# A Macaron block on one core: in steady passes the last shared chunk of a feed-forward layer is made behind the eleven expert chunks

## The reference

```python
x = x + 0.5 * ffn(_layernorm(x))          # pass f=0
x = x + mamba(_layernorm(x))              # state-space scan, 256 inner channels, 16 states
x = x + 0.5 * ffn(_layernorm(x))          # pass f=1, the same weights
```

```python
h = silu(einsum('tc,ech->eth', xf, W1)) * einsum('tc,ech->eth', xf, W2)
y = einsum('eth,ehc,te->tc', h, W3, w)    # w: the router's weight of each expert for a token
hs = silu(xf @ Ws1) * (xf @ Ws2)
y = y + (hs @ Ws3)
```

## Time and profile before

| | before |
|---|---|
| median of 3 runs | 1810.48 us (1804.98 to 1814.09) |
| the profiled execution | 1817.71 us |
| its span | 1816.0 us |
| mean granted TensorE clock | 0.975 |
| busy: PE, DVE, ACT, POOL | 1652.8, 1489.5, 1267.4, 1443.4 us |

### The profile page before, as it was taken

The page is one execution under the profiler, slowest core; times in us unless marked ns, Lnnn a source line. Parts: engine busy times, 40 slices in busy tenths (PEclk is TensorE's granted clock), DMA queues, the critical chain, the costliest instruction groups (busy, mean ns, idle before and its releaser), DMA issues.

```text
span 1816.0 us, 24043 instructions
## 1 busy us (share of the span) xinstructions
PE 1652.8 (91%) x7378; PEld 997.4 (55%) x7378; DVE 1489.5 (82%) x2244; ACT 1267.4 (70%) x2032; POOL 1443.4 (79%) x1362
## 2 busy tenths in 40 slices
PE   7878788999999999999999999999999999976689
PEld 4544445556565555556555555655555565543346
DVE  3177989889898988989798988989898898978862
ACT  3387678787868777776867777787777868585522
POOL 5256778888888888888888888889898888887853
PEclk9999889999999999999999999999999999988899
DMA  6127668686867778586777867777686868667732
GB/s 182 43 86 171 152 160 203 154 203 155 201 169 182 186 164 202 152 194 171 184 180 171 201 158 190 179 185 187 158 209 152 198 162 196 166 163 180 162 88 76
DMA packets 120999, 302.97 MB, mean 167 GB/s; under 512 B 19267, under 2 KB 40486, under 8 KB 106662
## 3 DMA queue, kind: packets, MB, share of 16 engines
q0 software_dynamic: 18144, 124.26, 34.2%
q1 hardware_dynamic: 100214, 175.36, 33.6%
q10 hardware_dynamic: 2512, 1.81, 0.3%
HBM read 167.67 MB, written 5.24 MB: 95 GB/s over the span
## 4 chain that ended last, share of the span: by engine, by line
POOL 45%; DMA 20%; issue 14%; PE 10%; DVE 8%; ACT 3%; SPq 1%; POOLq 0%; DVEq 0%; ACTq 0%
DMA yacc<-prod 18%; POOL prod L730 18%; POOL gated L661 14%; POOL yacc L726 3%; DVE hist L1023 3%; PE ps_y L1201 3%; DVE ps_db L978 2%; PE ps_h1a L1185 1%; PE ps_h2a L1209 1%; POOL yacc L747 1%; PE ps_h1b L1185 1%; PE ps_h2b L1209 1%; POOL xres L717 1%; POOL rstd L642 1%; POOL stdr L645 1%
## 5 line engine op out<-in xcount | busy, mean ns | idle before, releaser
L730 POOL TENSOR_TENSOR prod<-hist,crow 128x1024 f32<-128x1024 f32 x224 | 556.1, 2482 | 214.6 <-DVE hist L1023 183.8
L1201 PEld LDWEIGHTS ps_y<-down_w,gated 128*128 128x128 f32 (+1 forms) x3584 | 474.1, 195 | 278.9 <-issue 169.1
L1023 DVE TENSOR_TENSOR_SCAN hist<-decay,ps_db 128x1024 f32<-128x1024 f32 x256 | 583.5, 2279 | 3.0
L661 POOL TENSOR_TENSOR gated<-gated,silu 128x512 f32<-128x512 f32 x352 | 492.7, 1444 | 77.8 <-DVE gated L1003 74.3
L1201 PE MATMUL ps_y<-down_w,gated 128*128 128x128 f32 (+1 forms) x3584 | 489.1, 281 | 53.1 <-POOL gated L661 51.5
L978 DVE TENSOR_TENSOR ps_db<-du,ps_db 128x1024 f32<-128x1024 f32 x256 | 313.2, 1224 | 124.6 <-PE ps_db L1164 122.7
L791 ACT ACTIVATE decay<-delta,a_neg 128x510 f32<-128x510 f32 x512 | 326.8, 709 | 1.5
L808 ACT ACTIVATE silu<-ps_h1a 128x512 f32<-128x512 f32 (+1 forms) x224 | 133.0, 594 | 185.7 <-PE ps_h1a L1185 185.3
L1185 PE MATMUL ps_h1b<-xnT,up_w 128*128 128x512 f32 x448 | 238.6, 615 | 3.3 <-ACT silu L808 3.3
L1209 PE MATMUL ps_h2a<-xnT,up_w 128*128 128x512 f32 (+1 forms) x448 | 234.6, 606 | 6.6 <-DVE gated L1003 6.6
L1185 PE MATMUL ps_h1a<-xnT,up_w 128*128 128x512 f32 (+1 forms) x448 | 237.7, 612 | 0.0
(11 more groups left out here) (138 smaller groups left out, 1936.8 us busy)
## 6 DMA issues: line engine op xcount, KB each, us to landing
yacc<-prod POOLq DMA_DIRECT2D x111, 1024.0 KB, 9.8
crow<-c_rows SPq DMA_DIRECT2D x128, 512.0 KB, 5.0
wrow<-w_rows SPq DMA_DIRECT2D x320, 128.0 KB, 6.2
wrow<-w_rows SPq DMA_DIRECT2D x64, 224.0 KB, 7.1
wrow<-w_rows SPq DMA_DIRECT2D x64, 192.0 KB, 5.1
wrow<-w_rows SPq DMA_DIRECT2D x64, 160.0 KB, 2.8
yacc<-yacc POOLq DMA_DIRECT2D x15, 512.0 KB, 7.7
wrow<-w_rows SPq DMA_DIRECT2D x64, 96.0 KB, 2.9
```

The lines of the kernel that those rows point to most:

```text
L661: nc.gpsimd.tensor_tensor(gated[:, pos % NGATE, :], gated[:, pos % NGATE, :], silu[:, (pos + NCHUNK * f_parity(of, f)) % NSILU, :], ALU.mu ...
L730: nc.gpsimd.tensor_tensor(prod[:, (pair - 1 + odd) % 2, s % 2, :, :], hist[:, s % 2, :, :], c_all, ALU.mult).then_inc(prod_done, 1)
L1023: nc.vector.tensor_tensor_scan(hist[:, s % 2, :, :].rearrange("p h t -> p (h t)"), decay[:, s % NA, :, :, :].rearrange("p h b t -> p (h b ...
L1201: ins = nc.tensor.matmul(ps_y[:, t * C:(t + 1) * C], gated[0:rd, posd % NGATE, t * P:(t + 1) * P], down_w[0:rd, jd, :], start=(posd == 0 a ...
```

## The change

In f=0 passes of groups entering in iterations 2 to 13, and in f=1 passes of iterations 2 to 14, a second order holds: chunks 11 and 12, then the eleven expert chunks, then chunk 13. Expert chunk e now stands at place e + 2, and the 96 rows of chunk 13 at p13. All other passes keep the order of before. `UNIT`, `PLAN` and `SP_PLAN`, and so the slot of every place and the order of SP's list, stay as they are. The semaphore counts for the reuse of `wrow` and `silu`, and those that PE waits for, are worked out from the new order.

```diff
-    ORDER = list(range(ECHUNK, NCHUNK)) + list(range(ECHUNK))
+    SHARED_FIRST = list(range(ECHUNK, NCHUNK)) + list(range(ECHUNK))
+    ONE_SHARED_LAST = list(range(ECHUNK, NCHUNK - 1)) + list(range(ECHUNK)) + [NCHUNK - 1]
+
+    def order(it, f):
+
+        return SHARED_FIRST if it < FULL or (f and it >= G - 1) else ONE_SHARED_LAST
...
+    CHUNKS = [(it, f, j) for it, f in PASSES for j in order(it, f)]
+    def experts_of(n):
+        return sum(j < ECHUNK for _, _, j in CHUNKS[:n])
+    def taken_with(of, f, e):
+        return CHUNKS.index((of, f, e)) + 1
+    EXPERTS = [(it, f, j) for it, f, j in CHUNKS if j < ECHUNK]
...
-                n = fcount(k, f, NCHUNK, e if e >= NW else e - (NCHUNK - ECHUNK))
-                if n > 0:
-                    sp.wait_ge(h2_taken, n)
+                n = EXPERTS.index((k, f, e)) - NW
+                if n >= 0:
+                    sp.wait_ge(h2_taken, taken_with(*EXPERTS[n]))
...
-                    if u is not None and ORDER[u[2]] < ECHUNK:
+                    if u is not None and order(u[0], u[1])[u[2]] < ECHUNK:
...
-                        shared = NCHUNK - ECHUNK
-                        if NSILU <= pos < NSILU + shared:
+                        if n >= NSILU and CHUNKS[n - NSILU][2] >= ECHUNK:
                             act.wait_ge(h2_taken, n - NSILU + 1)
                         elif n >= NSILU:
-                            act.wait_ge(weighted, fcount(of, f, ECHUNK, pos - shared - (NSILU - 1 if pos >= NSILU else 0)))
+                            act.wait_ge(weighted, experts_of(n - NSILU + 1))
...
-                            pe.wait_ge(weighted, fcount(of, fd, ECHUNK, jd + 1))
+                            pe.wait_ge(weighted, experts_of(fcount(of, fd, NCHUNK, posd + 1)))
```

More of the change, by code:

```diff
@@ L799, in body @@
                         of, f, pos = u
-                        r = rows(ORDER[pos])
+                        r = rows(order(of, f)[pos])
                         n = fcount(of, f, NCHUNK, pos)
                         act.wait_ge(h1_full, n + 1)
-                        shared = NCHUNK - ECHUNK
-                        if NSILU <= pos < NSILU + shared:
+                        if n >= NSILU and CHUNKS[n - NSILU][2] >= ECHUNK:
                             act.wait_ge(h2_taken, n - NSILU + 1)
                         elif n >= NSILU:
-                            act.wait_ge(weighted, fcount(of, f, ECHUNK, pos - shared - (NSILU - 1 if pos >= NSILU else 0)))
+                            act.wait_ge(weighted, experts_of(n - NSILU + 1))
                         nc.scalar.activation(silu[0:r, (pos + NCHUNK * f_parity(of, f)) % NSILU, :],
@@ L989, in body @@
                         of, f, pos = u
-                        j = ORDER[pos]
+                        j = order(of, f)[pos]
                         r = rows(j)
@@ L1189, in body @@
                         of, fd, posd = d
-                        jd = ORDER[posd]
+                        jd = order(of, fd)[posd]
                         rd = rows(jd)
                         if jd < ECHUNK:
-                            pe.wait_ge(weighted, fcount(of, fd, ECHUNK, jd + 1))
+                            pe.wait_ge(weighted, experts_of(fcount(of, fd, NCHUNK, posd + 1)))
                         else:
```

## The result

The changed kernel has a median of 1861.35 us (1858.40 to 1863.15, 4 runs), the kernel before, now with one more run, 1812.28 us. The ratio is 1.0271, with a 95% interval of 1.0250 to 1.0293: 49 us slower. Forecast were 1858 us and 47 us, with a range of 1843 to 1882 us.

What follows compares the result with a forecast made beforehand. PE was busiest (91%), but late weight rows at p6 and p7 of f=0 were to set the period: 239.0 - 192.0 = 47 us over twelve periods, put on 1810.5 us, giving 1858 us, range 1843 to 1882.

Steps and rivals of the forecast that it cites:

- The bound and the rule: Steady periods, store to store: each lasts 88.3 us plus the time of p7's gate behind the store.
- POOL counted 0: POOL's steps moved to slots 22 and 4 cost 0; slot 22 had a 3.66 us gap.
- The pair of chunk 4 at p6: Weight rows needed at p6 of f=0 at +10.2 us behind the store, but landing at +10.9 to +17.4.
- The 3.4 us behind it: DVE from p6's gate to p7's: 4.8 us less 1.4 for `hot` no longer meeting a POOL product.
- The pair of chunk 5 at p7: Weight rows needed at p7 of f=0 land at +18.9 to +20.7 us, so p7 cannot start before about +19.8.
- The sum: Twelve p7 gates of f=0: 239.0 less 192.0 is 47 us later, 3.9 each, all of it period.
- clock term: PE's granted clock falling behind waits: 0 in the sum, 0 to 2 us per period in the range.
- DVE's wait for weight rows: DVE's gates: waits for `wrow` grow from 33.7 us to about 33.7 + 12 x 5, nearly all at p6 of f=0.
- the cover: Chunk 10's pair at p12: 0 to 1.5 us late, covered by 1.51 us of DVE idle time; price 0.
- The f=1 passes: Their pairs land before their gates even one place earlier; 0 to 1 us kept for each of thirteen passes.
- The loads come in their own time: Rival at p6 and p7: chunk 4 lands by +10.2, chunk 5 by +15.0, 12.0 us won, 1798 us; chance 0.03.
- The delay is absorbed: Rival: DVE, busy only 92 of 104.8 us, absorbs the 4 us, so no change, 1810 us; chance 0.04.

Runs made afterwards that it cites:

- a_split_w5: Changed kernel with the store split into issue and later wait, pairs of chunks 4 and 5 issued right behind the store; 1801.2 us, 0.9936 of before.
- b_split: Kernel before with the store split into issue and later wait, so it no longer holds SP's list; 1802.0 us, 0.9957 of before.
- b_split5: Kernel before with the store split into issue and later wait, timed again in more rounds; 1803.1 us, 0.9939 of before.
- f1_only: New order in the thirteen f=1 passes alone, f=0 keeping the order of the kernel before; 1812.4 us, 1.0004 of before.

## Why the prediction was right, step by step

**The bound and the rule.** A period was to be 88.3 us plus the time of p7's gate. Its means held in all kernels, to 0.4 us. It was found from periods of one trace that differ by themselves, and it is what turned a landing time into a time of the kernel. Where it does not hold is the twelfth pass (the paragraph under the table of experiments), which the prediction counted like the others.

**POOL counted 0.** Right: a_split_w5, which has all of POOL's moves, runs at the floor. In slot 22 the added step lies in the gap of the earlier trace rows, which shrank from 3.66 to 2.74 us (forecast 2.4). POOL's timeline of the changed kernel:

```profile
580.26 1.26 POOL L678 TENSOR_TENSOR gated<-gated,silu 128x512 f32<-128x512 f32 x1
584.26 2.37 POOL L747 TENSOR_TENSOR prod<-hist,crow 128x1024 f32<-128x1024 f32 x1 [2.74 <-DVE hist L1039]
```

**The pair of chunk 4 at p6.** Landings were to be at +10.9 to +17.4; the gate stood at +11.0 to +17.1. "At +14.7 at the earliest in a full period" missed once, at +12.3. The 3.4 us behind it measured 3.3. The choice against 4.8 rested on `hot`, which was to lose its 1.4 us once it no longer ran beside a POOL product. It took 0.23 us at 598.07 where it took 1.79 in the earlier trace rows. The 0.35 us that the prediction took as undisturbed still met the end of a product (last section), so the saving was 1.56 us and not 1.4.

**The pair of chunk 5 at p7.** Forecast from +18.9 to +20.7. It is seen alone where chunk 4 came early, in the period with its store at 1013.93:

```profile
1026.19 0.69 DVE L1019 TENSOR_TENSOR gated<-ps_h2a,wrow 128x512 f32<-128x512 f32 x1 [2.00 <-DMA wrow<-w_rows]
...
1034.00 0.69 DVE L1019 TENSOR_TENSOR gated<-ps_h2b,wrow 128x512 f32<-128x512 f32 x1 [3.78 <-DMA wrow<-w_rows]
```

p6 at +12.3, but p7 at +20.1, and that period took 108.4 us.

**The sum.** 239.0 was forecast for the twelve times of p7, 239.9 it was (12 x 19.99), against 191.9 before: 48 us. The medians say 49. In the traces the eleven full periods are 43.9 us longer, for 43.9 us at p7, and the twelfth only 2.1 us, for 4.0 at p7: 46.0 us in all. The forecast thus added the twelfth where the rule is not shown, a matter of 2 us here. The spans of the two profiled executions say only 40.7. Most of the rest is no gain of the change: the first store stands at 366.9 us in the trace of before and at 360.4 to 366.1 in all the others, at 362.9 and 363.6 in b_split and b_split5, whose order is that of before up to there. Start-up, with its own waits for loads, differs by some us from trace to trace.

**What was a little off.** The range's clock term was put at 0 to 2 us per period; it is 1.4 us in the whole steady part, and the same in the kernel before, so nothing in the difference (last section). DVE's wait for weight rows was to grow by some 5 us a period, from 33.7 to about 94 us; it is 101.3. DVE's waits in the steady part are 58.3 us at p6, 17.0 at p7 and 14.0 at p12, which cost nothing. The prediction had 0 to 1.5 us a period at p12 but left them out of that growth, and took 1.51 us as the cover, where 2.24 us was still covered. Of these waits 16.1 us are put down to PE in the profile; 73.6 of the 101.3 us are in the steady part (14.4 of 33.7 before), the rest in start-up and end. The f=1 passes were put at 0 to 1 us each; they show one wait of 0.29 us, and f1_only no loss. The idle time of PE was put at 6.5 us in four pieces; the period above shows 5.4, of which 5.0 in three.

**The rivals.** "The loads come in their own time" needed a landing by +10.2, and the earliest gate of p6 was at +11.0, just behind its landing. "The delay is absorbed" fell with the rule. The Trainium skill's fixed cost of about 2 us for one DMA (DMA: Bandwidth & Descriptors, "Anatomy of one DMA — SWDGE (gpsimd) path") is stated for a DMA issued by GpSimd, and the pairs here are issued by SP, among other loads; in the changed kernel the second half of chunk 4 took 5.1 us in the period with its store at 1013.93 and 7.4 us in that at 362.1. How much of that is queueing behind other transfers is not separated here.

## What to carry to other kernels

A reordering that moves no busy time can still move when an operand is needed: list the loads whose use comes earlier, and for each what holds its issue. That need not be the buffer: here it was something unrelated ahead of it in the same queue, a store that waits until it has landed. Where a period repeats with natural scatter, look for one event whose time goes one to one into the period; it prices a delay before a kernel is run, in the periods that are alike. What follows on another table, as the twelfth pass here, has to be priced by itself. And split a blocking store into issue and wait before reordering around it: that was worth 0.4 to 0.6% in the old order by itself.

## What the runs showed of the hardware that I had not expected

*An operation beside POOL.* `hot`, 128x64, took 0.22 or 0.23 us in ten of the twelve periods of the changed kernel (0.92 and 0.93 in the other two), away from the POOL product, and 1.79 us beside that product in the earlier trace rows. It was not slowed in proportion; it ended when the product did. POOL's timeline of the kernel before, the product beside each of the two `hot` rows:

```profile
1007.73 2.36 POOL L730 TENSOR_TENSOR prod<-hist,crow 128x1024 f32<-128x1024 f32 x1
...
962.87 2.37 POOL L730 TENSOR_TENSOR prod<-hist,crow 128x1024 f32<-128x1024 f32 x1 [1.78 <-DVE hist L1023]
```

The first product ends at 1010.09 and `hot` at 1010.17, the second product at 965.24 and `hot` at 965.32. In all eleven traces each `hot` that starts while a product runs ends 0.07 to 0.10 us behind it, whether it began early or late in it. A late DVE thus lost less than its delay, since `hot` no longer met the product: in the period shown above p6 was 6.1 us late and p7 only 4.6.

*The granted clock.* The changed kernel has a PE wait of 1.87 to 1.89 us at the down product of p7 in eight of twelve periods (0.29 to 0.93 in the others), and the clock left 1.00 in six of the first eleven, where it did so in two of eleven in the kernel before. Three of the periods (stretch, its length, busy PE, PEld, DVE, ACT and POOL, granted clock, DMA share, GB/s):

```profile
579.80:687.70 107.90, 100.64 (x463) 61.00 (x462) 90.98 (x139) 79.28 (x128) 89.78 (x85) 1.00 0.73 174
469.60:579.80 110.20, 103.67 (x463) 62.66 (x462) 91.08 (x139) 79.34 (x128) 89.74 (x85) 0.97 0.72 170
1446.70:1555.60 108.90, 103.05 (x463) 62.37 (x462) 91.02 (x139) 78.99 (x128) 89.73 (x85) 0.97 0.72 173
```

The second has its p7 at +21.2, should take 88.3 + 21.2 = 109.5 us and took 110.2. The third has the same mean clock and its p7 at +20.7, which makes 109.0, and took 108.9. Where the clock fell tells them apart. A pair of up products takes 1.02 us at 2.4 GHz and 2.08 at 1.2. PE's timelines, the second stretch first:

```profile
499.49 1.16 PE L1217 MATMUL ps_y<-down_w,gated 128*128 128x128 f32 x8 [1.88 <-POOL gated L678]
...
502.20 1.91 PE L1201 MATMUL ps_h1a<-xnT,up_w 128*128 128x512 f32 x2
```

```profile
1464.32 2.08 PE L1225 MATMUL ps_h2a<-xnT,up_w 128*128 128x512 f32 x2 [2.90 <-DVE gated L1019]
...
1470.39 1.02 PE L1225 MATMUL ps_h2b<-xnT,up_w 128*128 128x512 f32 x2
...
1475.98 1.16 PE L1217 MATMUL ps_y<-down_w,gated 128*128 128x128 f32 x8 [0.66 <-POOL gated L678]
```

In the second stretch PE is slow behind its wait at the down product, where nothing of its work is covered, and the period is 0.7 us longer. In the third it is slow behind the wait for the freed `ps_h2a`, ahead of that wait: the slow products use up idle time, and the wait at the down product shrinks to 0.66 us. Two of the six periods (stores at 469.6 and 687.7, the latter 108.2 us for 107.6) are 0.7 us over the rule, as the second stretch; the other four follow it, as the third. So the lower clock cost 1.4 us in the whole steady part, much less than the 0 to 2 us a period that I kept for it. The kernel before has two such periods too, with its stores at 470.16 and 1099.53, each 0.7 us over the rule, so in the difference of the two kernels the clock is nothing. The prediction's count for that kernel was also a little off: the twelfth period, at 0.95, was a third with a lower clock, and of the eight with a wait of 1.85 to 1.89 us at the down product of p7 six kept 1.00.

*A label that names the wrong engine.* In three periods of the changed kernel the wait at p6 is put down to PE, as in

```profile
376.97 0.69 DVE L1019 TENSOR_TENSOR gated<-ps_h2a,wrow 128x512 f32<-128x512 f32 x1 [4.64 <-PE ps_y L1217]
```

The PE product named is no input of this gate. The second half of chunk 4's pair was issued near 369.3, the second of two from 368.87 on in 0.96 us, and took 7.4 us to land, which is 376.7: it was the load. Summed by label, waits for `wrow` come out too small.
